# A perceiver on one core: the shares of the heads formed behind the cross attentions, experts' first weights fetched and split ahead, a recurrence worked by halves

## The reference, cut to what matters

```python
x = x + L0_xattn(ln(x), ctx)      # self attention + MLP, then 16-head cross attention + MLP ("a1", "a2")
x = x + L0_attn(ln(x))            # 16 heads, rotary                                        ("l0a")
x = x + L0_ffn(ln(x))             # 8 experts, 2 per token, + 2 shared halves, 352 wide      ("l0f")
x = x + L1_xattn(ln(x), ctx)      # one head                                                ("l1x")
x = x + L1_attn(ln(x))            # recurrence below                                        ("l1a")
x = x + L1_ffn(ln(x))             # 8 experts with a capacity                               ("l1f")
x = x + L2_xattn(ln(x), ctx)      # 16 heads of 64                                          ("l2x")
x = x + L2_attn(ln(x)); x = x + L2_ffn(ln(x))   # rotary; 8 experts + 1 shared, 256 wide    ("l2a", "l2f")
x = x + L3_xattn(ln(x), ctx)      # 16 heads of 16                                          ("l3x")
x = x + L3_attn(ln(x)); x = x + L3_ffn(ln(x))   # 16 experts + 6 shared parts, 128 wide     ("l3a", "l3f")

# cross attention, each head h:
a = softmax(q_h k_h^T * scale);  o_h = (a @ v_h);  out = concat(o_h) @ Wo
# gated experts: choose 2 of the experts by a softmax of x @ router
y = sum_e combine_e * ((silu(x @ W1_e) * (x @ W2_e)) @ W3_e)
# recurrence over the 64 tokens of a row (w = -exp(decay), u = first):
p = max(pp, u + k);  y = (e^(pp-p) aa + e^(u+k-p) v) / (e^(pp-p) bb + e^(u+k-p))
p2 = max(pp + w, k); aa = e^(pp+w-p2) aa + e^(k-p2) v;  bb = e^(pp+w-p2) bb + e^(k-p2);  pp = p2
out = (sigmoid(r) * y) @ Wo
```

## Time and profile before

| | us |
|---|---|
| median of 3 runs (lowest to highest) | 2496.91 (2496.58 to 2503.9) |
| the profiled execution, its own time | 2489.59 |
| its span, first to last instruction | 2487.8 |
| granted TensorE clock, mean of the span | 0.918 |

### The profile page before, as it was taken

One profiled execution on the slowest core, in us unless ns is written; L12 is line 12 of the kernel. 1 busy time (PEld: TensorE's weight loads), 2 busy tenths in 40 slices (PEclk: granted clock), 3 DMA queues, 4 the chain that ended last, 5 costly groups with the idle time before them and its releaser, 6 DMA issues. The chain is left out here.

```text
span 2487.8 us, 43407 instructions
## 1 busy us (share of the span) xinstructions
PE 2147.6 (86%) x15168; PEld 1795.9 (72%) x15168; DVE 1478.7 (59%) x3265; ACT 1185.5 (48%) x2419; POOL 469.2 (19%) x381
## 2 busy tenths in 40 slices
PE   4767999999886986359899999986989999999878
PEld 1645999999554863148599999954758998987567
DVE  6444877777334442551477777733446777776356
ACT  1234676676323431221476666632336666665244
POOL 2213212220012310000221221110322222210034
PEclk9788999999976997579899999995999999999779
DMA  4252101000002223412201010002121101000022
GB/s 195 60 204 93 41 28 42 27 27 0 34 11 85 83 106 151 173 53 102 77 31 39 28 41 27 0 2 79 63 83 41 42 28 41 27 14 1 11 67 81
DMA packets 32324, 145.41 MB, mean 58 GB/s; under 512 B 3760, under 2 KB 9136, under 8 KB 28848
## 3 DMA queue, kind: packets, MB, share of 16 engines
q1 hardware_dynamic: 32176, 143.53, 16.2%
HBM read 126.90 MB, written 13.90 MB: 57 GB/s over the span
## 5 line engine op out<-in xcount | busy, mean ns | idle before, releaser
L1098 DVE TENSOR_TENSOR pTl<-ps,pTh 128x512 fp32r<-128x512 f32 (+1 forms) x768 | 438.9, 584 | 114.3 <-ACT pTh L1014 113.4
L1014 ACT ACTIVATE pTh<-ps 128x512 fp32r<-128x512 f32 (+1 forms) x768 | 356.9, 519 | 195.1 <-PE ps L902 184.9
L589 PE MATMUL ps<-pTh,ch 128*128 128x256 f32 (+1 forms) x1248 | 383.3, 307 | 9.7 <-DVE pTl L1098 5.3
L590 PE MATMUL ps<-pTl,ch 128*128 128x256 f32 (+1 forms) x1248 | 348.7, 279 | 0.0
L591 PE MATMUL ps<-pTh,cl 128*128 128x256 f32 (+1 forms) x1248 | 348.3, 279 | 0.0
L589 PE MATMUL ps<-cTh,qh 128*128 128x512 f32 (+2 forms) x768 | 276.9, 361 | 15.2 <-POOL ql L856 8.0
L591 PE MATMUL ps<-cTh,ql 128*128 128x512 f32 (+2 forms) x768 | 269.1, 350 | 0.0
L590 PE MATMUL ps<-cTl,qh 128*128 128x512 f32 (+2 forms) x768 | 268.8, 350 | 0.0
L1085 DVE TENSOR_REDUCE top<-ps 128x1 f32<-128x802 f32 x192 | 189.4, 987 | 116.7 <-PE ps L591 116.7
L589 PEld LDWEIGHTS ps<-pTh,ch 128*128 128x128 f32 (+1 forms) x1248 | 235.1, 188 | 26.1 <-DVE pTl L1098 25.8
L590 PEld LDWEIGHTS ps<-pTl,ch 128*128 128x128 f32 (+1 forms) x1248 | 235.8, 189 | 0.1
(11 more groups left out here) (332 smaller groups left out, 3896.3 us busy)
## 6 DMA issues: line engine op xcount, KB each, us to landing
w<-l1f_w_in SPq DMA_DIRECT2D x16, 1024.0 KB, 9.0
raw<-ctxT_in SPq DMA_DIRECT2D x16, 801.0 KB, 4.3
raw<-ctx_in SPq DMA_DIRECT2D x14, 832.0 KB, 4.5
wg<-l0f_guide_in SPq DMA_DIRECT2D x10, 704.0 KB, 4.9
z<-ctx_in SPq DMA_DIRECT2D x8, 832.0 KB, 12.8
z<-z SPq DMA_DIRECT2D x8, 832.0 KB, 11.3
c<-ctx_in SPq DMA_DIRECT2D x8, 832.0 KB, 9.2
zT<-zT SPq DMA_DIRECT2D x8, 801.0 KB, 14.3
```

The costliest lines, as they stand in the source:

```text
L589: pe.matmul(out, high, moving_high, start=start, stop=False)
L590: pe.matmul(out, high, moving_low, start=False, stop=False)
L1014: nc.scalar.activation(pTh[0:w, PARTS[g][0]:PARTS[g][0] + n, slot, :], ps[0:w, turned_bank[slot][g], 0:n * P].rearrange("p (k r) -> p k r" ...
L1098: dve.tensor_tensor(pTl[0:w, at, slot, :], ps[0:w, turned_bank[slot][g], 0:n * P].rearrange("p (k r) -> p k r", r=P), pTh[0:w, at, slot, : ...
```

## The change

1. **Cross attention.** The exponentials add up into `sums`, one column per part and unit, at an index that the loop gives. `add_totals`, `invert_total`, `make_diag`, `spread_shares`, `keep_shares` and `scale_values` are gone. VectorE stores the value product from PSUM to q, not divided. A new `late_values` takes the place of `head_values`' dense: it inverts all totals at once, turns them by 16 small matmuls, splits them in halves, spreads them to the rows of a group of heads by a product with a picked identity, and multiplies each group's projection by it; in a2 the norm's bias enters as a column behind that.
2. **Experts.** `expert_weights` opens room for the first expert before the self attention, fetches its weights there, and `split_first` splits them on GpSimd during the self attention's last `rows_to_norms`. The router, the choice and the shared weights lie inside the experts' block; the choice stands on VectorE behind the low half of x and before the first gated product. `silu` lies in the rows' part of `normed`. The code of `route` is cut in `route_on_scalar` and `route_on_vector`, same instructions.
3. **Single head.** `one_head_keys` holds pairs 0 and 1 and fetches them before l0a; pairs 2 and 3 get room of their own and are fetched at the stage's start. Nothing is fetched in the attention.
4. **Recurrence.** One block for all. Mixing is ordered by k, v, r; products start with k; the scans and what follows work on one chunk of channels (a half) at a time; `fall` is made on ScalarE and GpSimd; three multiplications of each half go to GpSimd; the second maximum and two subtractions become one gap with a Relu to either side on ScalarE.
5. `inner` and `mid` have room for the whole program.

```diff
@@ cross_attention
+                                                 accum_out=sums[:, bass.ds(2 * v + half, 1)])\
...
+                        def store(c, batch, k):
+                            dve.wait_ge(value_ready, c + 1)
...
+                            if gain is None:
+                                dve.tensor_copy(dst, src).then_inc(value_kept, 1)
+                            else:
+                                dve.tensor_scalar(dst, src, gain, None, ALU.mult).then_inc(value_kept, 1)
@@ late_values, TensorE
+                        product(0)
+                        product(1)
+                        pe.wait_ge(inverted, 1)
+                        for b in range(B):
+                            for e in range(2):
+                                last = pe.matmul(ps[32 * e:32 * e + 32, 6, b * S:b * S + S], inverse[:, b, :],
+                                                 ident[:, e * S:e * S + S], start=True, stop=True)
+                        last.then_inc(rows_ready, 1)
...
+                        for m in range(2, M):
+                            product(m)
+                            if m == 2:
+                                pe.wait_ge(heads_ready, 1)
+                                pe.wait_ge(rows_low, 1)
+                            spread(m - 2)
+                        spread(M - 2)
+                        spread(M - 1)
@@ late_values, VectorE
+                        dve.tensor_tensor(total, halves[:, :, :, 0], halves[:, :, :, 1], ALU.add).then_inc(added, 1)
+                        dve.reciprocal(total, total).then_inc(inverted, 1)
+                        dve.tensor_tensor(rl[:], rows_psum, rh[:].bitcast(F32), ALU.subtract).then_inc(rows_low, 1)
+                        for m in range(M):
+                            dve.wait_ge(products, m + 1)
+                            dve.wait_ge(shares_kept, m + 1)
+                            dve.tensor_tensor(oT[:, m, :], ps[:, m % 4, :], share[:, m % 2, :], ALU.mult).then_inc(taken, 1)
@@ expert_weights
+                def split_first(pool):
+                    pool.wait_ge(guide_landed[0], 16)
+                    pool.tensor_copy(wgh[0][:], wg[0][:, 0:2 * KC * hidden]).then_inc(guide_high, 1)
+                    pool.wait_ge(guide_high, 1)
+                    pool.tensor_tensor(wgl[0][:], wg[0][:, 0:2 * KC * hidden], wgh[0][:].bitcast(F32), ALU.subtract)\
+                        .then_inc(guide_low, 1)
...
+                fetch_guide(nc.sync, 0, 0)
+                fetch_down(nc.sync, 0, 0)
@@ experts, VectorE
                         dve.tensor_tensor(xl[:], xT, xh[:].bitcast(F32), ALU.subtract).then_inc(x_low, 1)
+                        dve.wait_ge(logits_ready, 1)
+                        link(dve.tensor_copy(logits[:], logits_psum))
...
+                        route_on_vector(dve, link, room, logits[:, :, 0:routed], combine, kind, exp_wanted, exp_done)
...
                         in_order(first_product, second_product, dve.Fori)
@@ one_head_cross
+                for p in range(2, B // 2):
+                    context.hold(p, tmp)
+                    context.fetch(nc.sync, p)
@@ recurrence, GpSimd
+                        for c in range(KC):
+                            pool.wait_ge(exponents, 2 * c + 2)
+                            pool.wait_ge(v_kept, c + 1)
+                            pool.tensor_tensor(weighted[:, c, :], new[:, c, :], v[:, c, :], ALU.mult).then_inc(weighted_ready, 1)
...
+                            pool.tensor_tensor(boost[:, c, :], e_new[:, c, :], v[:, c, :], ALU.mult).then_inc(boosted, 1)
...
+                            pool.tensor_tensor(rated[:, c, :], num[:, c, 0:N], r[:, c, :], ALU.mult).then_inc(rated_ready, 1)
@@ recurrence, VectorE
+                        for c in range(KC):
+                            dve.wait_ge(k_kept, c + 1)
+                            link(dve.tensor_tensor_scan(top[:, c, 1:N + 1], fall[:, c, :], k[:, c, :], 0.0, ALU.add, ALU.max))
...
+                            link(dve.tensor_tensor(den[:, c, 0:N], den[:, c, 0:N], e_new[:, c, :], ALU.add))
+                            link(dve.reciprocal(keep[:, c, :], den[:, c, 0:N]))
@@ the order of the stages
+        with one_head_keys() as context:
+            context.fetch(nc.sync, 0)
+            context.fetch(nc.sync, 1)
+            gains = weights("l0a")
+            with expert_weights("l0f", 352) as held:
+                inner_attention("l0a", True, True, "bo", lambda t: plus(mid[:, t, :], xn[:, t, :]),
+                                [(mid, inner, (), (gains("gamma"), gains("beta"))), (x, xn, (inner,), None)],
+                                held.split_first)
+                gated_experts("l0f", 8, 10, 352, "pair", held)
+            one_head_cross(context)
```

More of the change, by code:

```diff
@@ L83, in chunks @@
         return self(name).rearrange("p (k n) -> p k n", k=n)
+OneHeadKeys = namedtuple("OneHeadKeys", "keysT keys landed hold fetch")
+ExpertWeights = namedtuple("ExpertWeights", "wg wgh wgl wd wdh wdl columns guide_landed down_landed guide_high guide_low "
+                                            "down_high down_low room fetch_guide fetch_down split_first")
+RoutePlaces = namedtuple("RoutePlaces", "count small eight index where first second row pair")
 ContextKeys = namedtuple("ContextKeys", "cTh cTl ch cl raw fetch_keysT fetch_keys")
@@ L808, in cross_attention @@
                 ntop = sb("ntop", [P, 2], where=own)
-                total = sb("total", [P, 2, 2], where=own)
-                rtotal = sb("rtotal", [P, 2], where=own)
-                diag = sb("diag", [P, 2, 2 * P], where=own)
-                share = sb("share", [P, 2 * P], where=own)
-                value = sb("value", [P, 2 * P], where=own)
                 flat = ps[:, 0:4, :].rearrange("p n k -> p (n k)")[:, BANK - LEAD:]
@@ L1042, in body @@
                                 before = not (first and u == 0)
-                                older = before and not (first and u == 2)
                                 if before:
@@ L1296, in second_product @@
                                 turn_tile(pe, NT - 1, xn, NT - 1, z_ready, turned_ready)
+                        for t in range(NT):
+                            for k in range(KC):
+                                last = pe.matmul(logits_psum[:, t, :], xT[:, k, t * P:(t + 1) * P], router[:, k, :],
+                                                 start=(k == 0), stop=(k == KC - 1))
+                        last.then_inc(logits_ready, 1)
                         pe.wait_ge(x_low, 1)
@@ L1473, in _ @@
-                        for t in range(NT):
-                            last = dve.max(eight[:, t, :], scores[:, t, :])
-                        link(last)
-                        for t in range(NT):
-                            last = dve.max_index(index[:, t, :], eight[:, t, :], scores[:, t, :])
-                        link(last)
-                        link(dve.tensor_copy(where_[:], index[:]))
-                        places = iota[:, 0:count].unsqueeze(1).broadcast_to([P, NT, count])
-                        dve.tensor_tensor(first[:], places, spread(where_[:, :, 0]), ALU.is_equal).then_inc(chain, 1)
@@ new lines, in recurrence @@
+                den = sb("den", [P, KC, N + 1], where=tmp)
+                gap, e_old, e_new = (mixed[:, m] for m in range(3))
+                weighted, boost, rated = fall, new, fall
+                names = ("chain", "scaled", "mixed_ready", "product_ready", "decay_ready", "fall_ready", "cleared", "k_kept",
+                         "v_kept", "r_kept", "arguments", "exponents", "gaps", "parts", "lifted", "den_scanned",
+                         "weighted_ready", "num_scanned", "boosted", "summed", "rated_ready")
@@ L2303, in perceiver_kernel @@
-        held, inner, mid = two_attentions()
-        with held:
-            gains = weights("l0a")
-            inner_attention("l0a", True, True, "bo", lambda t: plus(mid[:, t, :], xn[:, t, :]),
-                            [(mid, inner, (), (gains("gamma"), gains("beta"))), (x, xn, (inner,), None)])
-        plain = [(x, xn, (), None)]
-        gated_experts("l0f", 8, 10, 352, "pair")
-        one_head_cross()
-        with capacity_weights() as held_experts:
-            recurrence(held_experts[3])
-            capacity_experts(held_experts)
+            experts(held, weights(name).chunks("router", KC), routed, kind, total, hidden, bias, name != "l3f")
@@ L2314, in perceiver_kernel @@
+        with capacity_weights() as held:
+            recurrence(held[3])
+            capacity_experts(held)
         many_head_cross("l2x", 64, 64 ** -0.5, True)
-        inner_attention("l2a", True, False, "bu", add_to_x, plain)
-        gated_experts("l2f", 8, 9, 256, "all", bias=True)
+        with expert_weights("l2f", 256, True) as held:
+            inner_attention("l2a", True, False, "bu", add_to_x, plain, held.split_first)
+            gated_experts("l2f", 8, 9, 256, "all", held, bias=True)
```

769 lines of the change are left out of this document (410 added, 359 removed).

## The result

The changed kernel takes 2371.5 us (median of four runs, 2367.7 to 2373.7) against 2499.0 for the kernel before: ratio 0.9486, 95% interval 0.9465 to 0.9507. The prediction was 2378. The timed runs differ by 127.4 us, the two profiled executions by 116.7: that of the kernel before (2489.6) was 7 us faster than the fastest of its four timed runs. All tables by stage go by the profiled ones, and where the 10.7 us between lie can't be read from them.

A forecast was written before the change was run, and what follows sets the result against it. TensorE's own work bounds three cross attentions, chains of waits the glue between. Terms -56 + 19 - 38 - 22 - 22 = -119 us, from the median 2496.9 to 2378; range 2352 to 2414.

The forecast's parts named there:

- Part 1: Many-head cross attentions' loop: shares leave it, saving 0.43 us of records and 0.15 of waits per couple, 56 us gained.
- my 0.34: Cross attentions' loop: TensorE's waits for VectorE's low halves, 0.34 us per couple; all going was the upper bound, 74 us.
- Part 2: Behind the cross attentions' loops: the shares come back as late work, 19 us lost in all, bounds 10 to 30.
- Part 3: Experts' start: only the router stays ahead of the first expert matmul, 38 us net gained after 2 lost in l0a.
- Part 4: Single-head attention: earlier key fetches remove TensorE's waits of 21.2 us; 22 us gained, bounds 15 and 24.
- Part 5: Recurrence by halves: 29 us gained, less 7 for VectorE and GpSimd excluding each other; 22 net, bounds 14 and 30.
- Rival A: Cross attentions' loop gains nothing, as VectorE's and ScalarE's chain holds the 12.64 us period: 2434 us, chance 0.07.
- B: GpSimd and VectorE don't hinder each other, and all waits of the cross attentions' loop vanish: 2351 us, chance 0.15.
- C: Cross attentions' exponentials held back by register-given sum addresses; at 0.55 us each 19 us slower, 2516 us; chance 0.02.
- D: Moves only shift waits: late weights or keys, v's swap, table switches, late shares costing 30 us; 2410 us, chance 0.14.

The follow-up runs named there:

- run 1: Changed kernel with each couple's spread matmul (ones by a 128x256 tensor) put back into the cross attentions' loop, unused: 2416.5 us, 0.9699 of before.
- run 2: Changed kernel with VectorE's small sums, reciprocals and 128x128 products put back into the cross attentions' loop, unused: 2397.1 us, 0.9605 of before.
- run 5: Changed kernel with unused matmuls (14 in a2, 8 in l2x and l3x) behind the last spread of the late shares: 2362.8 us, 0.9474 of before.
- run 7: Changed kernel with expert 1's gate and up weights fetched ahead of the next stage's pack instead of behind it: 2365.3 us, 0.9479 of before.
- run 8: Changed kernel with expert 0's weights of l0f split at the experts' start again, not during l0a's output rows: 2372.2 us, 0.9501 of before.
- run 10: Changed kernel with expert 0's weights both fetched and split at the experts' start in all three stages: 2382.0 us, 0.9534 of before.
- run 9: Changed kernel with the single head's pairs 0 and 1 fetched at the start of l1x, together with 2 and 3: 2379.2 us, 0.9515 of before.
- run 6: Changed kernel with GpSimd's six products of the recurrence moved to VectorE: 2372.7 us, 0.95 of before.
- run 4: Changed kernel with exponentials' sums in four fixed columns and a constant for the totals' sums, so values stay undivided by real totals: 2365.1 us, 0.9488 of before.
- 11: Changed kernel with 12 unused matmuls in a2, 6 in l2x and l3x, and expert 1's gate and up weights fetched before the next pack: 2359.2 us, 0.945.
- 12: The changed kernel itself, unedited, timed again in the same rounds as 11: 2366.8 us, 0.948 of the kernel before.

## Why the prediction was right, and where it was not

**Part 1**, -56, measured -67 (bounds 0 to -74). The mechanism holds, the size is off in one term: the records cost 0.43 as read (0.42 in run 1, in l2x and l3x; in a2 it stays open), but VectorE's small work cost 0.28 us a couple (run 2) where I took 0.15. Of the waits I had read one row of two: with the transposes' 4.0 us they were 14.8 us in l3x, and 10.5 of these went, 0.34 a couple, which with the record's 0.42 is 0.76 of the 0.785 gained. That my 0.34 comes out all the same is luck. In the other two stages about 0.23 a couple is left beside 0.42. Those two had a shorter period before than l3x, the only one that I read.

**Part 2**, +19, measured +21 up to the rows and +10 behind them. The ends at 9.9 (l3x), 12.0 (a2) and 16.8 us (l2x) stand beside 10.5, 12 and 15. Two terms in them were off: the 32 small records took 1.1 us (I took 2.2), so that the first share spread 4.3 to 4.7 us in and not 5.6; and in l2x the groups follow each other every 1.66 us, TensorE's product and spread, not at VectorE's 0.7. The step that failed is the silent one, that the rows behind would take what they took before: around the wait ahead of them TensorE's clock halved (run 5). In a second profiled run of the same kernel that cost 4.5 us, not 10.

**Part 3**, -38, measured -37 in the experts and +2.7 in l0a. The first expert matmul comes 3.4 us behind the router's first (3.8). In l3f the choice ended 9.9 us in, not 11.5, and TensorE waited 0.35, not 2. "The first expert's matmuls cover" the second one's weights failed in l2f: ScalarE stood at their landing with the first silu behind it, and TensorE waited 2.3 us, which the edit of run 7 removed. And the reason that I gave for most of the gain was too narrow: the split ahead is worth 2.2 us in l0f (run 8), fetch and split 16 in all (run 10), router and choice beside other work 21.

**Part 4**, -22, measured -24.9. The waits of 21.2 are gone, and the warmer clock shortens the first pair's scores from 5.61 to 4.61 us, those of all pairs from 20.5 us to 14.4; the bound of 24 was too tight. That the early fetch of pairs 0 and 1 is needed is right for a reason that I didn't have (run 9).

**Part 5**, -22, measured -25.4. From first mix to the output's matmuls 36.7 us, forecast 40. Taking turns is shown, at 3.8 us instead of 7 (run 6): two of the six products fell almost wholly beside reciprocals, which kept 3.35. The Trainium skill ("SBUF — State Buffer", "Who interferes with whom") has it that a VectorE instruction with two SBUF inputs takes turns with a GpSimd instruction that reads SBUF, and that one with a single input doesn't, outside VectorE's 2-port modes. The trace agrees on the first, 1.75 us with the neighbour against 0.75 without, and for the reciprocal on the second, 3.35 both ways. But the prediction left out the page's condition and took the norms of l2a and l3a as free. In l2a one of their instructions is not, though it has a single tensor input:

```profile
1626.24 0.85 DVE L306 TENSOR_SCALAR normed<-x,mv,rstd 128x256 f32<-128x256 f32 x1
1629.39 0.41 DVE L306 TENSOR_SCALAR normed<-x,mv,rstd 128x256 f32<-128x256 f32 x1
```

The first runs beside GpSimd's split; in the profiled executions of runs 2, 4, 5, 7, 11 and 12 the same one took 0.71 to 0.73; in run 10 and before the change, both without the split there, none took more than 0.42. The price is 0.4 us at most.

**The sum.** In the profiled executions -119 stands against -116.7. Part 1 gave 11 us more and parts 4 and 5 gave 6 more; part 2 cost 2 more itself and 10 by the clock, part 3 with l0a brought 4 less, stages that the change doesn't touch lost 2, and 1.5 lie elsewhere in the attentions. Rival A is refuted (period 11.86), B half right (most of the waits went, the hindrance didn't), C refuted (run 4; its price for 0.55 us per exponential should by its own terms have been 96 x (2.2 - 1.84) = 35 us, not 19), and of D part 2 did cost about 30, but through the clock, which D doesn't name; its other terms didn't come.

## What to carry over

Work of an engine with time to spare is not free in a loop: what counts is whether it stands ahead of something that the bounding engine waits for. A new wait of TensorE can cost its length and then the clock of what follows; price both, and try unused matmuls in the wait. Fetch early, but count what SP has to issue: with twelve transfers issued in a row each further one took SP 1.7 us, and the next border that all engines pass together waited for it.

## What was not expected of the hardware

- The granted clock fell to 0.50 around waits of 1.8 us behind thin work (l2x, l3x) and 3.5 us (a2), and stayed at 1.00 when they were filled; in l2x it fell with six unused matmuls in the wait and 0.44 us idle; which stages run at half clock changes from run to run of the same instructions, by up to 10 us in l0a.
- An issue on SP mostly took 0.45 us for the first twelve transfers of 0.8 MB and 1.64 to 1.70 for the next four (run 9).
- A VectorE instruction with one tensor input was lengthened beside GpSimd's split, 0.41 to 0.85 us (l2a), while a reciprocal of one input was not (3.35 us both ways).
- An accumulated column whose address a register gives costs no more than a fixed one (0.938 us for an exponential, both ways).
